# Cross attention of a decoder layer: scores as three bf16 products, probabilities scaled by GpSimd

## The reference, cut to what matters

```
qx = _fp8_linear_pertensor(ln_out, wqx, ...).reshape(b, s, g, hpg, d)     # 8 groups, 2 heads each, d = 128
qx = _ln(qx, qxln_w, qxln_b)
kvx = einsum('bsi,oi->bso', cond, w_kv_x);  kx, vx = split(kvx, 2)
kx = _ln(kx.reshape(b, sc, g, d), kxln_w, kxln_b)                         # sc = 375
scores = einsum('bsghd,btgd->bghst', qx, kx) * scale
p = softmax(scores, axis=-1)
xout = einsum('bghst,btgd->bsghd', p, vx)
```

## Time and profile before

| | |
|---|---|
| median of 3 runs | 1215.86 us (1215.51 to 1218.77) |
| the profiled execution | 1215.43 us |
| its span in the profile | 1213.1 us |
| part A and the S halves | up to about 473 us |
| cross halves (L1000 runs) | 473 to about 1083 us |
| feed-forward | from about 1040 us to the end |

### The profile page before, as it was taken

How to read it: one execution, slowest core, us unless ns; L and a number is a source line. 1 busy time by engine, 2 the same in 40 slices (tenths; PEclk the granted TensorE clock), 3 DMA queues, 4 the chain that set the end, 5 groups by cost and what they waited for, 6 DMA issues and landing times.

```text
span 1213.1 us, 19327 instructions
## 1 busy us (share of the span) xinstructions
PE 1150.4 (95%) x6330; PEld 764.5 (63%) x6330; DVE 920.6 (76%) x2801; ACT 809.5 (67%) x2316; POOL 608.9 (50%) x769
## 2 busy tenths in 40 slices
PE   4889988789999999999999999999999999999998
PEld 2657756556666666666666766667666666554564
DVE  4668977999878876898999989987887546586252
ACT  4667658777878876677667766678776678566140
POOL 1546984653544555454566656444544112257172
PEclk9989989899999999999999999999999999999999
DMA  8220010211211221213232232226111000000000
GB/s 273 88 60 25 26 34 17 86 51 56 70 36 36 60 84 48 79 43 108 92 113 77 69 103 74 78 70 208 61 44 52 1 2 1 1 1 1 36 1 27
DMA packets 30788, 72.41 MB, mean 60 GB/s; under 512 B 3184, under 2 KB 12528, under 8 KB 30688
## 3 DMA queue, kind: packets, MB, share of 16 engines
q1 hardware_dynamic: 30416, 70.82, 18.5%
q10 hardware_dynamic: 272, 0.36, 0.1%
HBM read 62.78 MB, written 8.39 MB: 59 GB/s over the span
## 4 chain that ended last, share of the span: by engine, by line
PE 59%; DVE 19%; ACT 12%; POOL 7%; issue 1%; DMA 1%; ACTq 0%; POOLq 0%; SPq 0%
PE ps L901 14%; PE ps L1194 8%; PE ps L1122 8%; PE ps L891 7%; PE ps L1070 5%; PE ps L1000 4%; PE ps L1263 4%; ACT big L830 4%; PE ps L1035 3%; PE ps L841 3%; DVE big L415 2%; DVE big L1023 2%; POOL big L699 2%; DVE big L243 1%; POOL big L698 1%
## 5 line engine op out<-in xcount | busy, mean ns | idle before, releaser
L901 PE MATMUL ps<-big 128*125 128x512 bf16 x1152 | 264.6, 379 | 1.4 <-ACT big L830 1.3
L830 ACT ACTIVATE big<-ps,big 112x128 f32<-112x128 f32 (+1 forms) x512 | 192.8, 456 | 71.6 <-POOL big L433 68.9
L901 PEld LDWEIGHTS ps<-big 128*125 128x125 bf16 x1152 | 155.1, 136 | 81.9 <-ACT big L830 1.9
L432 POOL TENSOR_TENSOR big<-big 112x4 f32<-112x4 f32 (+1 forms) x128 | 37.5, 293 | 327.2 <-ACT big L427 327.1
L891 PE MATMUL ps<-big 128*112 128x512 bf16 x768 | 187.9, 388 | 5.4 <-ACT big L994 2.1
L891 PEld LDWEIGHTS ps<-big 128*112 128x112 bf16 x768 | 100.1, 133 | 70.7 <-issue 7.7
L1003 ACT ACTIVATE big<-ps,big 112x375 f32<-112x375 f32 x128 | 74.6, 583 | 91.0 <-DVE big L1002 90.3
L415 DVE BATCH_NORM_STATS2 big<-ps 112x6 f32<-112x128 f32 (+1 forms) x512 | 113.2, 283 | 20.3 <-PE ps L901 17.3
L1070 PE MATMUL ps<-big 125*128 125x224 f32 (+1 forms) x512 | 121.1, 359 | 5.3 <-DVE big L1052 4.3
L1023 DVE TENSOR_SCALAR big<-big 112x112 f32<-112x112 f32 (+1 forms) x256 | 120.0, 490 | 6.8
L1000 PE MATMUL ps<-big 128*112 128x375 f32 x256 | 102.1, 480 | 0.9 <-ACT big L830 0.9
(11 more groups left out here) (122 smaller groups left out, 2323.6 us busy)
## 6 DMA issues: line engine op xcount, KB each, us to landing
big<-in_ctx_t SPq DMA_DIRECT2D x32, 375.0 KB, 3.4
big<-in_w_s SPq DMA_DIRECT2D x16, 512.0 KB, 4.4
big<-in_w_p SPq DMA_DIRECT2D x16, 512.0 KB, 4.3
big<-in_w_x SPq DMA_DIRECT2D x16, 512.0 KB, 3.7
big<-in_w_g SPq DMA_DIRECT2D x16, 512.0 KB, 4.0
scr<-big SPq DMA_DIRECT2D x36, 128.0 KB, 1.7
big<-scr SPq DMA_DIRECT2D x9, 512.0 KB, 8.6
big<-in_w_d SPq DMA_DIRECT2D x8, 512.0 KB, 4.8
```

The source lines that it names most:

```text
L830: t = act(lambda e, j=j: e.activation(z[0:rows, 128 * j:128 * j + 128], bk[0:rows, 128 * j:128 * j + 128], ACT.Identity, bias=rr[0:rows, 4 ...
L901: t = pe(lambda e, k=k, s=s, u=u, n=n: e.matmul(bk[0:CK, :], cT[:, s, k, CK * c:CK * c + CK], w[:, u, k, col:col + 512], start=n == 0, sto ...
```

## The change

In the cross halves alone:

- q and k are kept as a high and a low bf16 part. `lnb_t` scales and adds the bias in place in the bank (f32), copies it as bf16 to SBUF (the high part, ScalarE), and a new stage `p_lo` (lag 4) subtracts the high part from the bank into the low one (VectorE). The bank is freed by `p_lo`, one tick later than before.
- A head's scores are three bf16 products into one bank: high by high, high by low, low by high.
- The scaling of the probabilities moves from VectorE to GpSimd, as a multiplication with the reciprocal broadcast over 375 columns. It frees the slot of `pr`.

The self halves keep their arithmetic; their q lies in the same ring and is only viewed in another way.

```
--- before.py
+++ after.py
@@ -189,7 +189,7 @@
         small = Ring([f32(rings.take(40), 40) for _ in range(5)])
         small2 = Ring([f32((consts if n < 2 else rings).take(8), 8) for n in range(5)])
         a_att = rings.at
-        qr = Ring([f32(rings.take(896), 896).rearrange("p (h t) -> p h t", h=8) for _ in range(2)])
+        qr = Ring([f32(rings.take(896), 896) for _ in range(2)])
         aCat = [rings.take(512), rings.take(512), aCX]
         cats = [b16(a, 1024).rearrange("p (h t) -> p h t", h=8) for a in aCat]
         pr = Ring([f32(rings.take(376), 376) for _ in range(2)])
@@ -801,7 +801,7 @@
         vS = Ring([f32(aKV + a, 512).rearrange("p (c n) -> p c n", c=1) for a in (1920, 896, 1408)])
         X_K1, X_V1 = aKV, aKV + 1500
         X_CT, X_K0, X_V0 = aKV + 3036, aKV + 4536, aKV + 6036
-        kX = Ring([f32(a, 1500).rearrange("p (g t) -> p g t", g=4) for a in (X_K0, X_K1)])
+        kX = Ring([b16(a, 3000).rearrange("p (s g t) -> p s g t", s=2, g=4) for a in (X_K0, X_K1)])
         vX = Ring([f32(a, 1536).rearrange("p (c n) -> p c n", c=3) for a in (X_V0, X_V1)])
         ctr = Ring([b16(X_CT, 3000).rearrange("p (s k t) -> p s k t", s=2, k=4)])
 
@@ -834,6 +834,11 @@
             small.release(it["si"], t)
             it.update(z=z, zi=zi, tz=t)
 
+        def q_view(q, S):
+            if S:
+                return q.rearrange("p (h t) -> p h t", h=8)
+            return q.bitcast(BF).rearrange("p (s h t) -> p s h t", s=2, h=8)
+
         def lnb_t(it):
             rows, z = it["rows"], it["z"]
             bi, (bk, _), free = bank.take()
@@ -844,6 +849,12 @@
             w, bb = it["wb"]
             dst, free_dst = it["dst"]()
             b3 = bk[:, 0:4 * rows].rearrange("p (g t) -> p g t", g=4)
+            if it["batch"]["k"] == "X":
+                hi, lo = dst
+                tf = act(lambda e: e.activation(b3, b3, ACT.Identity, bias=bb, scale=w), t, t_qsb)
+                th = act(lambda e: e.activation(hi, b3, ACT.Copy), tf, free_dst)
+                it["low"] = (bi, b3, hi, lo, th, free_dst)
+                return
             tf = act(lambda e: e.activation(dst, b3, ACT.Identity, bias=bb, scale=w), t, free_dst, t_qsb)
             bank.release(bi, tf)
             it["batch"]["ready"] += [tf]
@@ -937,7 +948,10 @@
                     if c == 0:
                         bt["q"] = qr.take()
                     _, q, qf = bt["q"]
-                    return q[:, 4 * c:4 * c + 4, :], qf
+                    q = q_view(q, S)
+                    if S:
+                        return q[:, 4 * c:4 * c + 4, :], qf
+                    return (q[:, 0, 4 * c:4 * c + 4, :], q[:, 1, 4 * c:4 * c + 4, :]), qf
             else:
                 o = V_KW if S else V_KXW
                 it["wb"] = (vc[:, o:o + 1], vc[:, o + 1:o + 2])
@@ -951,12 +965,19 @@
                     _, kk, kf = bt["kk"]
                     if S:
                         return kk, kf
-                    return kk[:, :, CK * c:CK * c + CK], kf
+                    return tuple(kk[:, s, :, CK * c:CK * c + CK] for s in range(2)), kf
             it["dst"] = dst
 
         def p_t(it):
             if it["what"] != "v":
                 lnb_t(it)
+
+        def p_lo(it):
+            if "low" in it:
+                bi, b3, hi, lo, th, free = it["low"]
+                tl = dve(lambda e: e.tensor_tensor(lo, b3, hi, ALU.subtract), th, free)
+                bank.release(bi, tl)
+                it["batch"]["ready"] += [th, tl]
 
         def att_items():
             items = []
@@ -997,8 +1019,10 @@
                         accum_out=sm[0:T, 2 + hh:3 + hh]), tm, pf)
             else:
                 h = 2 * g + it["hh"]
-                t = pe(lambda e: e.matmul(bk[0:T, 0:SC], q[:, h, :], kk[:, g, :], start=True, stop=True),
-                       bt["ready"], free)
+                for n, (s, u) in enumerate(((0, 0), (0, 1), (1, 0))):
+                    t = pe(lambda e, n=n, s=s, u=u: e.matmul(
+                        bk[0:T, 0:SC], q[:, s, h, :], kk[:, u, g, :], start=n == 0, stop=n == 2),
+                        bt["ready"], free, signal=n == 2)
                 tm = dve(lambda e: e.tensor_reduce(sm[0:T, 0:1], bk[0:T, 0:SC], AX.X, ALU.max, negate=True), t, mf)
                 te = act(lambda e: e.activation(p[0:T, 0:SC], bk[0:T, 0:SC], ACT.Exp, bias=sm[0:T, 0:1],
                                                 accum_out=sm[0:T, 2:3]), tm, pf)
@@ -1016,12 +1040,14 @@
             ri = sm[0:T, 4:4 + n]
             tr = dve(lambda e: e.reciprocal(ri, sm[0:T, 2:2 + n]), it["te"])
             hi_i, hl, hf = hlr.take()
-            for j in range(n):
-                dst, src = hl[0:T, w * j:w * j + w], p[0:T, w * j:w * j + w]
-                if S:
-                    dst, src = dst.rearrange("p (a n) -> p a n", a=7), p_head(p, j)
-                tl = dve(lambda e, j=j, dst=dst, src=src: e.tensor_scalar(
-                    dst, src, ri[:, j:j + 1], None, ALU.mult), tr, hf)
+            if S:
+                for j in range(2):
+                    tl = dve(lambda e, j=j: e.tensor_scalar(
+                        hl[0:T, w * j:w * j + w].rearrange("p (a n) -> p a n", a=7), p_head(p, j), ri[:, j:j + 1],
+                        None, ALU.mult), tr, hf)
+            else:
+                tl = pool(lambda e: e.tensor_tensor(hl[0:T, 0:w], p[0:T, 0:w], ri.broadcast_to([T, w]), ALU.mult),
+                          tr, it["te"], hf)
             pr.release(it["pi"], tl)
             small2.release(it["mi"], tl)
             it.update(hl=hl, hli=hi_i, tl=tl)
@@ -1331,7 +1357,7 @@
             u["free"] = lambda: a_end
         spill_ring = Ring([f32(a, 256) for a in (aFR, aFR + 256, aCX, aCX + 256)])
         order = [("p", 1, p_stats), ("p", 1, p_vhi), ("a", 3, t_s2), ("a", 0, t_s0), ("p", 1, p_rstd), ("a", 5, t_s4),
-                 ("p", 3, p_t), ("b", 6, b_4), ("b", 3, b_2), ("a", 1, t_s1), ("p", 1, p_z), ("a", 8, t_s6),
+                 ("p", 4, p_lo), ("p", 3, p_t), ("b", 6, b_4), ("b", 3, b_2), ("a", 1, t_s1), ("p", 1, p_z), ("a", 8, t_s6),
                  ("a", 4, t_s3), ("p", 0, p_mm), ("b", 2, b_m), ("b", 4, b_3), ("b", 1, b_1), ("b", 0, b_0)]
         every = tuple(range(8))
         beat = {LEAD + 7: every, LEAD + 39: every, LEAD + 71: (4, 5, 6, 7), 64 + LEAD: (0, 1, 2, 3),
```

8 lines of the change are left out of this document (6 added, 2 removed).

## The result

The changed kernel takes 1250.8 us (median of 4 runs, 1250.0 to 1254.3) against 1215.9 us (1215.5 to 1218.8) beside it: ratio 1.029, interval 1.0274 to 1.0307. It is slower by 35 us, 15 us more than forecast and inside the range. The profiled span is 1249.7 us.

A forecast was written before the change was run, and what follows sets the result against it. TensorE's work was taken to set the time, other engines close behind. Seven heavy batches +23 us, three lighter +3, the first +0.5, the last five -5.5, together +21 on 1215.4: 1236 us, range 1205 to 1254.

The forecast's parts named there:

- the three waits: Exp for its pr slot (0.9 us late), transposes for GpSimd's multiplication (1.9), projection for its bank (1.3 and 1.4).
- the rival of the clock: New waits lower TensorE's clock in heavy batches, 7 to 10 times 1.7 us on top: 1250 us; chance 0.14.
- Step 1: Scores on TensorE: three bf16 products take 0.476 us instead of 0.63, giving back 19.7 us over 128 heads.
- the load of weights: Rival: weight loads of the score products do not hide, +31 us instead of -19.7, about 1260 us; chance 0.03.
- a closer spacing: Rival: score products spaced by weight load alone, 0.40 us for three, gaining 30 us: 1226 us; chance 0.02.
- Step 2: VectorE: scalings go (5.24 us a batch), subtractions come (3.24); gains 2.0 us a batch, worth nothing directly.
- Step 3: ScalarE: added bf16 copies of q and k groups, 0.537 and 0.59 us each, 2.85 us a batch.
- Step 4: GpSimd: 8 multiplications a batch at 1.0 us, queued behind weight preparation (L372, L373), late for TensorE's transposes.
- Step 5: Two new waits: exp for its pr slot (0.9 us late); projection for a bank L830 reads (1.3 and 1.4).
- model batch: Cross-part batch from 590.8 to 628.8 us, used to estimate the seven heavy batches; about +3.6 us forecast.
- Absorbed: Rival: the multiplication's lateness is absorbed by lighter VectorE and slack, only the score saving counts: 1196 us; chance 0.13.
- half absorbed: Rival: each heavy batch loses 1.3 us net, not 3.3, as GpSimd's operations shrink: 1219 us; chance 0.12.

The follow-up runs named there:

- e6: Changed kernel with scaling back on VectorE and no low parts; one ScalarE step writes bf16, all three products use high parts: 1205.8 us.
- e2: Kernel before the change, f32 scores kept, with only the cross part's scaling moved to GpSimd: 1250.1 us, ratio 1.0285.
- e7: e6 with a second ScalarE step: affine step in place in the bank, then the bf16 copy, bank freed in the same tick: 1211.5 us.
- e10: Changed kernel with a third slot in the ring of exp results (pr): 1237.0 us, ratio 1.0175.
- e8: e7 with the bank given back one tick later, where p_lo stood, and no subtraction: 1222.0 us, ratio 1.0048.
- e12: Kernel before the change, with high and low parts and three bf16 products in three light batches alone: 1214.1 us, ratio 0.999.
- e1: Changed kernel with the scaling of the cross part's probabilities back on VectorE: 1227.9 us, ratio 1.0101.
- e9: Changed kernel with p_lo called first in its tick, lag 4 as before: 1262.0 us, ratio 1.038.
- e3: Changed kernel with p_lo right behind the copy it reads, in the same tick: 1371.5 us, ratio 1.1288.

## Why the prediction held, and which terms did not

The direction, the two engines and the three waits were right. The size was not: +20 was forecast, +35 measured, and the range held because it had been drawn wide enough for the rival of the clock, which is not what happened.

**Step 1, the scores.** The price is right. Chain of after:

```profile
630.31 0.48 PE ps L1023 x3
```

0.48 us for the three products, so neither the load of weights nor a closer spacing showed. The term of -19.7 was mis-sized as a gain of the kernel: alone it gave 9.4 (e6), and nothing in the seven heavy batches. The step that failed here is "TensorE's work sets the time here". It was read from busy times, 37.73 of 38.00; the chain of the same trace goes through VectorE, ScalarE and GpSimd in that batch, and in e6 it is the same chain, and the same length, with TensorE's work reduced.

**Step 2, VectorE.** The subtractions cost as estimated (0.616 and 0.669 us against 0.616 and 0.67). The other step that failed is "VectorE gains 2.0 us a batch", -32 us in all; measured is +9.2 over the kernel. Groups by form in the cross part, before:

```profile
L380 DVE SCALAR_TENSOR_TENSOR big<-big 128x256 uint32<-128x256 uint32 x48 | 21.8, 454 | 2.1 <-POOL big L373 2.1
...
L369 DVE TENSOR_SCALAR big<-big 128x512 bf16<-128x512 bf16 x48 | 15.5, 323 | 19.0 <-ACT big L359 18.0
...
L349 DVE TENSOR_SCALAR big<-big 128x256 uint32<-128x256 uint32 x47 | 13.9, 297 | 2.8 <-ACT big L329 2.8
```

and after:

```profile
L380 DVE SCALAR_TENSOR_TENSOR big<-big 128x256 uint32<-128x256 uint32 x48 | 34.8, 724 | 0.8 <-POOL big L373 0.8
...
L978 DVE TENSOR_TENSOR big<-ps,big 128x500 bf16<-128x500 f32 x45 | 30.1, 669 | 2.7 <-ACT big L855 2.5
...
L369 DVE TENSOR_SCALAR big<-big 128x512 bf16<-128x512 bf16 x48 | 25.0, 521 | 26.8 <-ACT big L359 26.8
...
L349 DVE TENSOR_SCALAR big<-big 128x256 uint32<-128x256 uint32 x47 | 21.7, 462 | 6.1 <-ACT big L329 5.0
```

The same operations on the same shapes take 13.0, 9.5 and 7.8 us more, 30 us together. L370, L243 and L674 take another 11 us more, and that makes up the 41 us between -32 and +9.2. The prediction had the sign of this ("every other one meets more GpSimd work") and priced it at under a microsecond a batch; these three lines alone are 1.9. The Trainium skill, "Advanced Engine Details and Errata", section VectorE Performance Modes, says that GpSimd and VectorE's 2-port instructions block each other, and section GPSIMD Details adds VectorE operations with two SBUF inputs. The trace agrees: L369, L349 (one SBUF input and output) and L380 (two SBUF inputs) grew, and L978, which reads a bank, stayed at the 0.616 us of its like in the earlier trace rows. L371, with two SBUF inputs, has nearly the same mean in both, 0.556 us and 0.551, but not because GpSimd leaves it alone: it takes 0.42 us in most ticks and up to 1.27 before and 2.03 after. Nor is it always the same line that pays. In e2, with as many multiplications on GpSimd, L369 stays at 0.33 us, and L380 and L370 go to 0.89 and 0.98 (0.45 and 0.81 before). Which VectorE operation is slowed depends on which one meets GpSimd's, so a mean by line does not carry over to another order.

**Step 3, ScalarE.** The copies took 0.544 and 0.593 us against 0.537 and 0.59. They were worth 5.6 us of the kernel (e7), where the step counted 0.4 us in one wait.

**Step 4, GpSimd.** The multiplication took 0.87 us in the mean, not 1.0. The one that was to make TensorE wait 1.9 us made it wait 1.86. In after the chain over the seven heavy batches has 89 us of GpSimd, 8 before.

**Step 5, the new waits.** Both are there: the slot (66.0 us of ScalarE, worth 14 by e10) and the banks (27 waits of the projection; e8 has them alone, +10.5). In the model batch the two first waits of L912 were forecast as 1.3 and 1.4 us and are 1.23 and 0.79 by idle time; the 0.8 us in the next batch did not come.

**The sum.** The model batch's own terms, 5.4 less 1.23 and 0.3, make 3.9 us, not the 3.6 written, and 3.3 was taken. Seven batches +23, measured +26.3, which is 3.8 each. Three up to 890, forecast +3, measured +6.5. First +0.5, measured +2.0. Last five -5.5, measured +1.1: this is the largest miss. The term "no such work, so they keep the gain" looked at GpSimd alone. Two of the five keep it (-1.2 us each) and one comes out even (+0.1), but one is 1.9 us longer, the batch in which e12 shows ScalarE's copy late, and the first of the five, in which GpSimd is still busy for some 24 us, is 1.6 longer. e1 and e2 keep these two apart. The batch of the late copy is 1.8 us longer in e1, which has the copies, and not in e2. The first of the five is 1.4 us longer in e2, which has the multiplications, and 0.4 in e1. Together +35.9 in the cross part against +21.

**The rivals.** Absorbed (heavy batches under 37 us) and half absorbed (1.3 us more than before, about 39.3) fell: they are 41.7 in the mean. The clock's rival gave the right time, 1250 us, for the wrong reason; that is luck. The windows of the model batch do show a fall (start:end, length, then as in the earlier trace rows):

```profile
627.00:633.00 6.00, 4.13 (x19) 2.58 (x18) 5.93 (x9) 2.89 (x6) 5.48 (x6) 0.85 0.25 65
633.00:639.00 6.00, 6.00 (x28) 3.39 (x27) 2.67 (x7) 4.97 (x10) 4.15 (x5) 0.87 0.62 195
```

but it is the only one in the cross part, and the kernel before has one as well. After a wait of 1.86 us TensorE ran at its 1.2 GHz level for a while, and 12 products took 4.28 us instead of 12 x 0.216 = 2.59:

```profile
631.22 4.28 PE ps L912 x12
```

Worse orders do bring the rival's mechanism (5 falls in e9, 23 in e3).

## What to carry to other kernels

Before moving an operation to a less busy engine, follow two things besides its busy time: what it frees (a slot, a bank) and who waits for that, and which operations of the other engines run slower beside it. A saving on the busiest engine is worth only what the next engine leaves: ask in each stage how many microseconds the second is behind, and read the chain of waits there, not the busy shares alone: a batch in which TensorE was busy for 37.73 of 38.00 us had a chain without it. A buffer held one tick longer can cost more than the operation for which it is held (10.5 us against 5.9 here).
